# k and the probabilities transposed by DMA, and the q product in two PSUM banks in turn

## What is computed

```
q = rmsnorm(LN(x) @ Wq) * gq ; k = rmsnorm(ctx @ Wk) * gk ; v = ctx @ Wv      # 16 heads of 128
x = x + softmax(q k^T / sqrt(128)) v @ Wo
h = silu(bit_linear(LN(x), w_gate)) * bit_linear(LN(x), w_up)                 # 8-bit x, ternary w
x = x + bit_linear(rms_norm(h) * ln_weight, w_down)
```

## Time and profile before

| | us |
|---|---|
| median of 3 runs | 586.13 (585.00 to 586.45) |
| the profiled execution | 585.11 |
| its span, first to last instruction | 583.3 |
| granted TensorE clock, mean | 0.958 of full speed |

### The profile page before, as it was taken

How to read it: one execution, slowest core, us unless ns; L and a number is a source line. 1 busy time by engine, 2 the same in 40 slices (tenths; PEclk the granted TensorE clock), 3 DMA queues, 4 the chain that set the end, 5 groups by cost and what they waited for, 6 DMA issues and landing times.

```text
span 583.3 us, 15141 instructions
## 1 busy us (share of the span) xinstructions
PE 470.0 (81%) x4968; PEld 372.8 (64%) x4968; DVE 494.0 (85%) x1125; ACT 455.1 (78%) x1495; POOL 328.3 (56%) x310
## 2 busy tenths in 40 slices
PE   0168375699999999999999999999998656668674
PEld 0156254588787877878788787878887532445453
DVE  3878889688988889888898888989889759999995
ACT  0269477599999999999999999999998545667573
POOL 1028335456766667677676677767777405545452
PEclk9989689799999999999999999999999995999899
DMA  7931401000000000000000000000000000000001
GB/s 292 333 96 51 166 1 34 4 1 1 0 0 0 0 0 0 0 0 0 0 0 0 0 0 0 0 0 2 2 3 1 1 2 1 9 26 21 18 29 46
DMA packets 10156, 16.60 MB, mean 28 GB/s; under 512 B 784, under 2 KB 7952, under 8 KB 9616
## 3 DMA queue, kind: packets, MB, share of 16 engines
q1 hardware_dynamic: 9024, 13.11, 6.8%
q10 hardware_dynamic: 1104, 3.15, 1.5%
HBM read 14.16 MB, written 2.10 MB: 28 GB/s over the span
## 4 chain that ended last, share of the span: by engine, by line
PE 40%; DVE 23%; issue 20%; POOL 9%; ACT 5%; DMA 1%; DVEq 1%; POOLq 0%; ACTq 0%
PE EB L340 10%; PE KQ L340 9%; PE SO L340 9%; PE TK L1050 3%; DVE pT L745 3%; POOL qshl L465 3%; POOL work L453 2%; DVE ham L866 2%; PE TM L1060 2%; DVE stage L936 2%; DVE kT L811 2%; DMA xs<-in_x 1%; PE TM L1026 1%; DVE wqs L877 1%; DVE qse L816 1%
## 5 line engine op out<-in xcount | busy, mean ns | idle before, releaser
L578 ACT ACTIVATE work<-SO,nbias,rq 128x128 f32<-128x128 f32 x256 | 114.3, 465 | 19.6 <-DVE nbias L784 15.3
L340 PE MATMUL KQ<-hT,wqs 128*128 (+1 forms) x1536 | 100.6, 224 | 15.9 <-DVE wqs L710 12.1
L459 POOL TENSOR_TENSOR rk<-kse,negh 128x4 f32<-128x4 f32 x64 | 65.3, 1021 | 85.1 <-DVE kse L776 85.1
L340 PEld LDWEIGHTS KQ<-hT,wqs 128*128 128x128 f16 x1536 | 94.5, 100 | 18.4 <-DVE wqs L710 7.7
L447 POOL TENSOR_TENSOR rq<-qse,negh 128x4 f32<-128x4 f32 x64 | 65.1, 1017 | 62.3 <-DVE qse L816 62.3
L340 PE MATMUL EB<-As,ohl 128*128 128x256 f16 x768 | 94.1, 272 | 0.0
L340 PEld LDWEIGHTS EB<-As,ohl 128*128 128x128 f16 x768 | 70.3, 97 | 8.6
L465 POOL TENSOR_TENSOR qshl<-work,qshl 128x512 f16<-128x512 f32 x64 | 74.1, 1158 | 0.0
L765 DVE SCALAR_TENSOR_TENSOR qhl<-KQ,gcol,qhl 128x512 f16<-128x512 f32 x64 | 48.0, 750 | 29.1 <-ACT qshl L551 28.1
L453 POOL TENSOR_TENSOR work<-work,rinv 128x512 f32<-128x512 f32 x64 | 66.5, 1039 | 6.8 <-DVE rinv L741 6.8
L558 ACT ACTIVATE kjunk<-KQ 128x128 f16<-128x128 f32 x256 | 68.0, 302 | 0.0
(11 more groups left out here) (158 smaller groups left out, 1049.5 us busy)
## 6 DMA issues: line engine op xcount, KB each, us to landing
xs<-in_x SPq DMA_DIRECT2D x4, 512.0 KB, 9.8
wvo<-in_wo SPq DMA_DIRECT2D x1, 2048.0 KB, 18.6
out<-wqs SPq DMA_DIRECT2D x16, 128.0 KB, 1.7
raw<-in_ctxT ACTq DMA_DIRECT2D x1, 1024.0 KB, 6.4
stage<-in_wk SPq DMA_DIRECT2D x1, 1024.0 KB, 12.5
stage<-in_wq SPq DMA_DIRECT2D x1, 1024.0 KB, 15.7
stage<-in_wq ACTq DMA_DIRECT2D x1, 1024.0 KB, 13.9
stage<-in_wgT SPq DMA_DIRECT2D x1, 1024.0 KB, 4.9
```

Of the source, the lines that this page charges most:

```text
L340: last = matmul(out, lhsT=left(i), rhs=right(j), start=start and n == 0, stop=stop and n == 2)
L459: pool.tensor_tensor(rk[:, s, :], kse[:, s, :], negh[:, 0:HG], ALU.pow).then_inc(rk_ok, 1)
L578: ins = act.activation(pe[:, s, c], SB[:, c], ACT.Exp, scale=rq[:, (g - AT_S) % 4, h:h + 1], bias=nbias[:, s, h:h + 1], accum_out=psm[:, s ...
```

## The change

1. k: VectorE writes the scaled k as before; ScalarE copies it as the float16 high half khl (one step later), VectorE subtracts to get the low half, and SP issues a DMA that transposes both halves (8 blocks of 128 x 128, 256 KB) from SBUF to SBUF into kT. TensorE's four transposes and VectorE's two passes over TKf (L801, L811) are gone.
2. Probabilities: VectorE scales them (pn, before on GpSimd) and makes the high half; GpSimd makes the low half; a second DMA of 256 KB transposes them into pT. TensorE's four transposes, L542 and L745 are gone.
3. SP's queue issues for each step pT of group t-3, then kT of group t, each behind waits for its low half and for the product that last read the buffer. The loads of the feed-forward weights and of ln_weight stand inside this sequence, at t = 4 and t = 16.
4. The q product goes to QB for even groups and to TKf, which is free, for odd ones; it waits for the low half of q two groups back instead of one.
5. On TensorE the context product stands last in the step; its high half is taken at the start of the next step by ScalarE and VectorE (offset AT_E), ahead of the q passes.
6. The written-out part has 12 steps instead of 8 (LOOP_B = 3). Five splits instead of three come before step 0; statistics, layer norms, their transposes, the splits of the context and the sums for the ternary weights are spread over steps 0 to 11.

```diff
-AT_SSQ, AT_TK, AT_S, AT_TP, AT_O, AT_E = 1, 2, 3, 4, 5, 6
+AT_SSQ, AT_S, AT_O, AT_E = 1, 3, 5, 6
-LN_AT = {"start": (0, 2), 0: (2, 4), 3: (4, 6), 4: (6, 7), 5: (7, 8)}
+LN_AT = {"start": (0, 2), **{i + 2: (i, i + 1) for i in range(2, 8)}}
+LOOP_B = 3
+        def q_bank(g):
+            return QB if g % 2 == 0 else TKf
-        SPLIT_AT = {"start": (0, 3), 0: (3, 5), 1: (5, 7), 2: (7, 9), 4: (9, 10), 5: (10, 11), 6: (11, 12)}
+        SPLIT_AT = {"start": (0, 5), 0: (5, 7), 1: (7, 9), 4: (9, 10), 5: (10, 11), 6: (11, 12)}
...
+            for t in range(NT + 3):
...
+                if t >= 3:
+                    k = t - 3
+                    sp.wait_ge(plo_ok, k + 1)
+                    if k >= 2:
+                        sp.wait_ge(o_ps, k - 1)
+                    sp.dma_start_transpose(pT[:, k % 2, :, :].rearrange("p a (h n) -> p (a h) n", h=HG),
+                                           phl[:, k % 2, :, :].rearrange("p a n -> p (a n)")).then_inc(pT_in[k % 2], 16)
+                if t < NT:
+                    sp.wait_ge(klo_ok, t + 1)
+                    if t >= 2:
+                        sp.wait_ge(s_ps, t - 1)
+                    sp.dma_start_transpose(kT[:, t % 2, :, :].rearrange("p a (h n) -> p (a h) n", h=HG),
+                                           khl[:, t % 2, :, :].rearrange("p a n -> p (a n)")).then_inc(kT_in[t % 2], 16)
...
                 if live(b, g, 4):
                     s = (g - 4) % 2
-                    need(pool, rinv_ok, b, g, 4)
-                    need(pool, pT_ps, b, g, 4, 2)
-                    pool.tensor_tensor(heads(pn[:, s, :]), heads(pe[:, s, :]), spread(rinv[:, s, :], SKV),
-                                       ALU.mult).then_inc(pn_ok, 1)
+                    need(pool, phi_ok, b, g, 4)
+                    need_dma(pool, pT_in[s], b, g, 4, 2)
+                    pool.tensor_tensor(phl[:, s, 1, :], pn[:, s, :], phl[:, s, 0, :],
+                                       ALU.subtract).then_inc(plo_ok, 1)
...
+                if live(b, g, 1):
+                    s = (g - 1) % 2
+                    need(act, kn_ok, b, g, 1)
+                    need_dma(act, kT_in[s], b, g, 1, 2)
+                    act.copy(khl[:, s, 0, :], kn[:, s, :]).then_inc(khi_ok, 1)
...
+                    dve.scalar_tensor_tensor(out=heads(pn[:, s, :]), in0=heads(pe[:, s, :]), scalar=P_SCALE,
+                                             in1=spread(rinv[:, s, :], SKV), op0=ALU.mult,
+                                             op1=ALU.mult).then_inc(pn_ok, 1)
...
+                    dve.tensor_copy(phl[:, s, 0, :], pn[:, s, :]).then_inc(phi_ok, 1)
...
+                    dve.tensor_tensor(khl[:, s, 1, :], kn[:, s, :], khl[:, s, 0, :], ALU.subtract).then_inc(klo_ok, 1)
...
-                    need(te, qlo_ok, b, g, 0, 1)
+                    need(te, qlo_ok, b, g, 0, 2)
...
-                            ins = pairs(te.matmul, QB[:, h * SQ:(h + 1) * SQ], lambda i: wqs[:, i, k, c],
+                            ins = pairs(te.matmul, q_bank(g)[:, h * SQ:(h + 1) * SQ], lambda i: wqs[:, i, k, c],
...
-                    for h in range(HG):
-                        c = slice(h * P, (h + 1) * P)
-                        ins = te.transpose(TKf[:, c], kn[:, s, c], ident_f[:, :])
-                    ins.then_inc(kT_ps, 1)
...
-                        ins = te.transpose(TPf[:, c], pn[:, s, c], ident_f[:, :])
-                    ins.then_inc(pT_ps, 1)
```

More of the change, by code:

```diff
@@ L153, in build_program, with ln_bank @@
         A_banks = (OB, EB[:, :], TPf, SB)
-        LN_banks = (TKf, TPf, OB, EB[:, :])
+        LN_banks = (TKf, TPf)
+        def q_bank(g):
+            return QB if g % 2 == 0 else TKf
+        def ln_bank(i):
+            return LN_banks[i] if i < 2 else TPf
         x_in = [sem(f"x_in{i}") for i in range(B // XB)]
@@ L198, in build_program @@
         khi_ok = sem("khi_ok")
-        kT_ps = sem("kT_ps")
-        kT_ok = sem("kT_ok")
+        klo_ok = sem("klo_ok")
+        kT_in = [sem(f"kT_in{i}") for i in range(2)]
         q_ps = sem("q_ps")
@@ L215, in build_program @@
         phi_ok = sem("phi_ok")
-        pT_ps = sem("pT_ps")
-        pT_ok = sem("pT_ok")
+        plo_ok = sem("plo_ok")
+        pT_in = [sem(f"pT_in{i}") for i in range(2)]
         o_ps = sem("o_ps")
@@ L299, in steps @@
         def steps(eng, step, ffn):
-            straight(step, 0, 2 * G)
-            with eng.Fori(2, 2 + F_CHUNKS) as b:
+            straight(step, 0, LOOP_B * G)
+            with eng.Fori(LOOP_B, LOOP_B + F_CHUNKS) as b:
                 for g in range(G):
                     step(b, g)
-            straight(step, G * (2 + F_CHUNKS), FFN_AT)
+            straight(step, G * (LOOP_B + F_CHUNKS), FFN_AT)
             for s in range(G):
@@ L335, in need, with need_dma @@
                 eng.wait_ge(s, b * G + k)
+        def need_dma(eng, s, b, g, off, back=0):
+            k = g - off - back
+            if isinstance(b, int):
+                if G * b + k >= 0:
+                    eng.wait_ge(s, 16 * ((G * b + k) // 2 + 1))
+            else:
+                eng.wait_ge(s, b * (8 * G) + 16 * (k // 2 + 1))
         def pairs(matmul, out, left, right, start, stop):
@@ L466, in step @@
                                        ALU.subtract).then_inc(qslo_ok, 1)
[L467 to L470, removed]
+                if now(b, g) in C_AT:
+                    c_low(C_AT[now(b, g)])
+                if now(b, g) == 3:
+                    roots(1, B // XB)
                 if now(b, g) == PREP_AT:
@@ L582, in step @@
                 A_out(now(b, g))
-                if now(b, g) in range(B // XB):
-                    c_high(g)
+                if now(b, g) + 1 in C_AT:
+                    c_high(C_AT[now(b, g) + 1])
                 if now(b, g) in range(3, 7):
@@ L713, in _ @@
             split("start")
-            statistics(1)
             def A_max(n):
@@ L735, in step @@
             def step(b, g):
-                if now(b, g) == 0:
-                    layernorm(XB, 2 * XB)
                 if live(b, g, 4):
@@ L955, in ln_transposes @@
                     te.wait_ge(h_ok, 2 * i + 2)
-                    bank = LN_banks[LN_BANK[i]]
-                    if i >= 6:
+                    bank = ln_bank(i)
+                    if i >= 2:
                         te.wait_ge(hlo_ok, i)
@@ L976, in step @@
                         te.wait_ge(w_lo, 3 + 2 * g)
-                    if now(b, g) == 2 * G - 1:
+                    if now(b, g) == LOOP_B * G - 1:
                         te.wait_ge(w_lo, CT_SPLIT)
@@ L994, in step @@
                     s, r = (g - AT_S) % 2, (g - AT_S) % 4
-                    need(te, kT_ok, b, g, AT_S)
+                    need_dma(te, kT_in[s], b, g, AT_S)
                     need(te, qlo_ok, b, g, AT_S)
@@ L1021, in step @@
                         te.wait_ge(Ascl_ok, 1)
-                    if not isinstance(b, int) and g == 0:
+                    if now(b, g) == LOOP_B * G - 1:
                         te.wait_ge(wscl_ok, 1)
@@ L1086, in ffn @@
                     te.wait_ge(x1_ok, B)
-                if now(b, g) == AT_T:
-                    te.wait_ge(kT_ok, NT)
                 if now(b, g) == AT_GU:
```

189 lines of the change are left out of this document (82 added, 107 removed).

## The result

| | before | changed |
|---|---|---|
| median, us | 586.20 (584.65 to 588.72, 16 executions) | 589.74 (587.09 to 594.45, 16 executions) |
| ratio to before | | 1.0064, 95% interval 1.0044 to 1.0084 |
| profiled execution, us | 585.1 (span 583.3) | 588.4 (span 586.5) |

The account below looks back on a forecast made before the run. Three engines in a tight ring, ScalarE and TensorE tightest, bound the kernel; 5.2 us gained in 52 even steps, 6 at the start, 3 lost at the end: 8.2 off 585.1, median 578, own range 570 to 584 (80%: 568 to 622).

Parts of the forecast that it names:

- VectorE's ring: Loop step: VectorE's own work, about 5.05 us, plus 0.45 waiting for GpSimd's rk, gives 5.5, under 5.90.
- rival B: Loop: VectorE and GpSimd hold each other up, step about 6.05 us, total 586, or 592 without start gain; chance 0.13.
- The ring without TensorE: Loop: ScalarE and VectorE hand-overs sum to 5.69 us a step, 5.90 with ScalarE's weight chunks; 5.90 also forecast after the change.
- the worth of TensorE's relief: Loop: removing eight transposes frees 0.87 us of TensorE a step, but gains only 0.10, what the next ring leaves.
- The new instructions: Loop step, ScalarE and VectorE: k copy 0.70 us, probability scaling 0.68, their high half 0.41, low half of k 0.68 to 0.75.
- rival A: SP's queue: DMA transposes become the bound, each step as long as two of them; 613 us at 3.25 each; chance 0.26.
- the sign set for it: DMA transposes taking over 2.95 us each would decide for the DMAs as bound; under 3 us landing fits the forecast.
- the high bound: DMA transpose: 1024 packets of 256 bytes at 0.070 us over 16 engines, 4.5 us each, 9.0 a step.
- The written-out steps: First 12 steps, before the loop: extra work spread over 12 steps instead of 8 gains 6 us (16 gained to 5 lost).
- 139 was the sign: Start of the loop: the k scaling of step 12 begins by 139 instead of 145 us if the start is right.
- The end: Emptying after the last steps: the last three groups' DMAs lie on the path, 3 us lost (0 to 8).

Follow-up runs that it names:

- the experiment with the swap: Against the changed kernel, VectorE's low half of k (L845) moved behind the scaling of the next k (L849): 621.37 us, ratio 1.0614 to the kernel before.
- the second execution: The changed kernel run again, unaltered, beside the experiments: 589.66 us, ratio 1.0067 to the kernel before, profiled span 588.2 us.

## Why the prediction was wrong

**The step that failed** is VectorE's ring in the part by part, "about 5.05 + 0.45 = 5.5, under 5.90": the wait for rk was sized with rk at 1.01, so that its stretch beside the low half of k stood in the sum at nothing. With it goes the 0.13 given to rival B. B had the mechanism, its place and nearly its size: a step of 6.05, 586 or 592; measured 6.04 and 589.7. The prediction held the row that shows it, rk at 1.46 behind a VectorE instruction with two SBUF operands, and the order of the new code, in which the low half of k starts just before rk; it was filed as a rival although nothing in the rows spoke against it. Term by term, per step of the loop: busy 51.23/60 x 6.04 = 5.16 (5.05 taken; L880 at 0.58 instead of 0.41, once in 4 steps, is 0.04 of the difference), wait for rk 0.66 (0.45 taken), and 6.04 - 5.16 - 0.66 = 0.22 of smaller gaps (none taken). The ring is 0.54 longer than taken, of which the last two terms are 0.43. That B came within 0.01 of the step is in part luck: it took a wait of 0.45 + 0.46 = 0.91 and 0.09 for the uneven lines, where 0.66 and 0.22 were measured (0.90 is the wait in the 33 steps that have one, and nothing in the others). The prediction also read its row slightly wrong: at 87.86 us L710 has 0.58 to go, not 0.46, and rk ends 0.88 after L710, not its own 1.01. That the blocked rk is the cause is shown by the kernel with k in PSUM: the same order, rk at 1.01, step 5.79. The Trainium skill, SBUF — State Buffer, section Who interferes with whom, states the exclusion; the trace agrees in both directions, 1.01 to 1.45 for GpSimd's small instruction here and 0.68 to 1.03 for VectorE's in the experiment with the swap, and with one operand in PSUM rk keeps its 1.01.

**The ring without TensorE, 5.90.** This was not a bound. Its 5.69 is a sum of distances from start to start along a closed path through one step, and such a sum is the length of that step whichever path is taken; it can't show how much shorter the step would be without TensorE. The kernel with k in PSUM does a step in 5.79. The 0.10 as the worth of TensorE's relief was too small a bound as well: putting the time back costs 0.17. By the kernels with rk unblocked, 6.00 to 5.79 is 0.21 a step, twice the forecast 0.10; the blocked rk adds 0.25, which gives the 6.04.

**The new instructions** came as taken: copy of k 0.692 (0.70), scaling of the probabilities 0.692 (0.68), their high half 0.427 (0.41), low half of k 0.683 (0.68 to 0.75):

```profile
L603 ACT CAST khl<-work x64: 627/692/750, 44.6 to 453.7; 128x512 f16<-128x512 f32 x64
...
L774 DVE SCALAR_TENSOR_TENSOR work<-work,rinv x64: 691/692/1654, 66.3 to 468.3; 128x512 f32<-128x512 f32 x64
L781 DVE CAST phl<-work x64: 426/427/1265, 67.1 to 469.0; 128x512 f16<-128x512 f32 x64
...
L845 DVE TENSOR_TENSOR khl<-work,khl x64: 671/683/693, 46.8 to 456.6; 128x512 f16<-128x512 f32 x64
```

The maxima of 1.65 and 1.27 are in the steps written out, where both start while GpSimd's 128x512 instruction L466 runs (L774 at 122.05, 0.04 after it; L781 at 103.22, with 0.98 of it to go). That L781, with one SBUF operand, is held up too is read from this one place. TensorE's busy time fell by 43 us (some 50 expected).

**The DMAs (rival A)** were hidden, but the sign set for it misread. Part 3 and part 6 of the page, as in the earlier trace rows:

```profile
q1 hardware_dynamic: 144192, 46.68, 37.9%
...
kT<-khl SPq DMA_TRANSPOSE x64, 3.1
pT<-phl SPq DMA_TRANSPOSE x64, 3.3
```

They land 3.1 and 3.3 us after issue, above the 2.95 from which A was to decide, and nothing came of it. The error is in A's condition: landing time is latency, not the time for which the engines are taken. The packets of the queue rose by 144192 - 9024 = 135168, that is 1056 a transpose, close to the 1024 of the high bound; but their time rose only by 0.379 x 586.5 - 0.068 x 583.3 = 183 us, 1.43 us a transpose, 2.9 of the 6.04 us step. The high bound of 4.5 had taken the packet at 0.070 us as in the loads, whose packets hold 1.45 KB in the mean (13.11 MB in 9024); a packet of a transpose holds 0.25 KB (33.57 MB in 135168) and takes 183 x 16 / 135168 = 0.022 us. A chance of 0.26 and an upper end at 622 rested on that. The Trainium skill, Advanced Engine Details and Errata, section X-Bar Transpose (TRN2), gives 350 to 400 GB/s, by which the prediction estimated 0.7 us to move 256 KB; here the measurement decides: 262144 bytes in 1.43 us of all engines are 183 GB/s.

**The written-out steps** gained 1.4 us (2.1 in the second execution), not 6; step 12 began at 145.3, where 139 was the sign. The term is mis-sized. The waits from 40 to 146 us:

```profile
PEld KQ L358 <- DVE work L849: 19.3, 8, 4.8
ACT work L610 <- DVE nbias L835: 17.9, 9, 4.7
...
DVE work L849 <- POOL rk L491: 5.9, 8, 0.9
```

Here, too, rk is blocked, 5.9 us in 8 steps, and the hand-overs with waits of up to 4.8 us are still there: from step 0 to step 12 VectorE is idle 16.1 of 105.2 us, where it was idle 19.1 of 106.6 in the same 12 steps before. So 3.1 us of idle time went, and 1.7 us more of busy time took more than half of them back. The prediction's third was of the 15.9 idle us of 8 steps. That the long waits come from the new split of the work alone was not tried.

**The end**: 3 us lost was forecast; one execution gains 0.5, the other loses 2.5. In the stretch from step 63 to the end (columns as in the earlier trace rows) the two executions of the same kernel differ in the granted clock and in TensorE's busy time, and not in VectorE's:

```profile
452.90:586.50 133.60, 86.26 (x547) 56.27 (x547) 113.53 (x290) 76.29 (x131) 57.95 (x42) 0.92 0.11 29
```

```profile
451.70:588.20 136.50, 91.70 (x547) 58.13 (x547) 113.51 (x290) 76.32 (x130) 57.90 (x41) 0.87 0.11 28
```

The first is the changed kernel, the second the same kernel run beside the experiments. That the clock (0.92 against 0.87 of its 2.4 GHz on average) makes the whole difference of 2.9 us is argued from these two rows, not shown.

## What to carry to other kernels

Before an instruction with two SBUF operands is put next to one on which another engine waits, look on the timeline for what GpSimd starts at that point: a row that shows one such stretched pair is a price, to be put in the sum and not among the rivals. The remedy that worked here is to let one of the two operands lie in PSUM (12 us of 590), where a bank has come free; changing the order of the two instructions cost 32 us. And ask of a DMA's number whether it is latency or occupancy: landing times are held against the slack of the consumer, the queue's share against the step.

## What was not expected of the hardware

- A GpSimd instruction of 128x4 elements waits out a whole VectorE instruction of 128x512 with two SBUF operands (1.01 to 1.45 us, with the start 0.10 us later), though it moves next to nothing. In these 33 steps of the loop rk starts between 0.01 us before L845 and 0.10 after it, and ends 1.54 to 1.56 us after L845's start in all of them, that is 0.87 after L845's 0.68; the missing 0.14 of its own 1.01 is, by estimate, what it does before it is held. In the other direction the low half of k beside GpSimd's 128x512 instruction went from 0.68 to 1.03, while behind a started 128x4 one (270.96 and 271.61 in the timeline above) it kept its 0.68.
- A VectorE instruction with one SBUF input is touched as well: L880, 0.415 in the kernel before, takes 0.577 where it starts (164.40) while GpSimd's 128x512 instruction L497 (163.55, 1.15 us) still runs; in the kernel with the swap, where L497 is over by then (165.41, 1.16 us, against 167.23), it takes 0.410:

```profile
L880 DVE TENSOR_SCALAR raw<-stage x12: 408/410/415, 167.2 to 456.4; - x12
```

- 256 KB of 16-bit elements transposed from SBUF to SBUF by DMA cost SP 1.23 us to issue, land 3.1 to 3.3 us later and take 1.43 us of all 16 DMA engines; with those engines busy at 91% the step did not change. One issue:

```profile
257.97 1.23 SPq L423 DMA_TRANSPOSE pT<-phl  x1
```
